# Sums of four key tiles for the softmax denominators, a third score bank, and normalising on GpSimd, in an attention and feed-forward block

## The reference

```
def _tc_rmsnorm(x, t, gw, gb, bw, bb):
    g = (t @ gw.T + gb)[:, None, :]
    b = (t @ bw.T + bb)[:, None, :]
    inv_rms = rsqrt(mean(x * x, axis=-1, keepdims=True) + EPS)
    return g * x * inv_rms + b

def _attention(x, Wq, Wk, Wv, Wo):
    q, k, v = heads of x @ Wq.T, x @ Wk.T, x @ Wv.T
    attn = einsum('blhd,bmhd->bhlm', q, k) / sqrt(dh)
    p = softmax(attn, axis=-1)
    o = einsum('bhlm,bmhd->blhd', p, v).reshape(B, L, D)
    return o @ Wo.T

def _swiglu(x, gate_w, hid_w, out_w):
    return silu(x @ gate_w.T) * (x @ hid_w.T) @ out_w.T

x1 = x + _attention(_tc_rmsnorm(x, t, g1w, g1b, b1w, b1b), Wq, Wk, Wv, Wo)
y  = x + x1 + _swiglu(_tc_rmsnorm(x1, t, g2w, g2b, b2w, b2b), gate_w, hid_w, out_w)
```

## Time and profile before

| | us |
|---|---|
| median of 3 runs | 2556.25 |
| lowest and highest | 2555.16, 2558.97 |
| profiled execution | 2545.35 |
| span of the profiled execution | 2543.2 |

### The profile page before, as it was taken

How to read it: one execution, slowest core, us unless ns; L and a number is a source line. 1 busy time by engine, 2 the same in 40 slices (tenths; PEclk the granted TensorE clock), 3 DMA queues, 4 the chain that set the end, 5 groups by cost and what they waited for, 6 DMA issues and landing times. The chain is left out here.

```text
span 2543.2 us, 39928 instructions
## 1 busy us (share of the span) xinstructions
PE 2382.3 (94%) x11396; PEld 1578.0 (62%) x11396; DVE 1710.1 (67%) x2732; ACT 1310.6 (52%) x2287; POOL 1108.1 (44%) x1063
## 2 busy tenths in 40 slices
PE   5999989999989999989999875999999999999999
PEld 4644436544437444447444344888888888888887
DVE  4766744666735766736667536887787778877877
ACT  3356662556662566653656734436344534453444
POOL 0255551355550555541555534650464147316611
PEclk8999999999999999999999997999999999999999
DMA  6212213212112222132122153115511542154125
GB/s 200 53 40 56 52 30 105 45 43 63 51 31 87 51 52 54 46 92 52 39 53 51 47 166 116 51 33 163 195 57 54 165 166 59 60 173 150 50 75 174
DMA packets 92655, 209.62 MB, mean 82 GB/s; under 512 B 15632, under 2 KB 15632, under 8 KB 90640
## 3 DMA queue, kind: packets, MB, share of 16 engines
q1 hardware_dynamic: 91344, 202.71, 27.2%
q0 software_dynamic: 1088, 4.19, 0.5%
HBM read 134.23 MB, written 19.92 MB: 61 GB/s over the span
## 5 line engine op out<-in xcount | busy, mean ns | idle before, releaser
L410 POOL TENSOR_TENSOR sums<-probs 128x512 f32<-128x512 f32 x512 | 653.3, 1301 | 791.7 <-ACT probs L558 789.2
L632 DVE TENSOR_REDUCE pmax<-bank 128x1 f32<-128x512 f32 x1024 | 654.7, 684 | 282.0 <-PE bank L842 271.0
L558 ACT ACTIVATE probs<-bank 128x512 f32<-128x512 f32 x1024 | 584.5, 597 | 398.7 <-PE bank L926 365.4
L926 PE MATMUL bank<-qs,ks 128*128 128x512 f32 x1024 | 458.0, 452 | 29.2 <-ACT probs L558 28.6
L842 PE MATMUL bank<-ks,qs 96*128 96x512 f32 x1024 | 403.3, 407 | 25.5 <-DVE pmax L632 25.4
L926 PEld LDWEIGHTS bank<-qs,ks 128*128 128x128 f32 x1024 | 191.0, 187 | 369.5 <-ACT probs L558 225.0
L1489 PE MATMUL bank<-H_hi,wt_hi 128*128 128x512 f32 x896 | 350.0, 391 | 14.8 <-DVE H_lo L1344 14.6
L1503 PE MATMUL bank<-ow,aw 128*128 128x512 f32 x1536 | 358.6, 392 | 0.0
L1489 PE MATMUL bank<-H_lo,wt_hi 128*128 128x512 f32 x896 | 349.3, 390 | 0.0
L1489 PE MATMUL bank<-H_hi,wt_lo 128*128 128x512 f32 x896 | 349.3, 390 | 0.0
L1503 PEld LDWEIGHTS bank<-ow,aw 128*128 128x128 f32 x1536 | 285.6, 188 | 59.8 <-issue 1.2
(11 more groups left out here) (135 smaller groups left out, 3138.3 us busy)
## 6 DMA issues: line engine op xcount, KB each, us to landing
raw<-in_gu_w SPq DMA_DIRECT2D x66, 512.0 KB, 3.6
wo_raw<-in_out_w SPq DMA_DIRECT2D x128, 256.0 KB, 2.8
ks<-qk_hi SPq DMA_DIRECT2D x136, 128.0 KB, 2.4
qs<-qk_hi SPq DMA_DIRECT2D x264, 64.0 KB, 2.0
x<-in_x SPq DMA_DIRECT2D x10, 1024.0 KB, 5.7
ks<-qk_lo SPq DMA_DIRECT2D x68, 128.0 KB, 2.4
qs<-qk_lo SPq DMA_DIRECT2D x132, 64.0 KB, 2.0
wv<-wv_parts SPq DMA_DIRECT2D x4, 2048.0 KB, 8.7
```

The lines of the kernel that those rows point to most:

```text
L410: nc.gpsimd.tensor_tensor(sums[:, h, :], probs[:, 0, h, :], probs[:, 1, h, :], ALU.add) \
L558: nc.scalar.activation(probs[:, s % 2, h, :], sbank[i % SB][:], ACT.Exp, scale=SCALE).then_inc(st_done, 1)
L632: nc.vector.reduce_max(pmax[:, t, h, hf:hf + 1], mbank[n % MB][:], AX_X).then_inc(sq_done, 1)
L926: nc.tensor.matmul(sbank[i % SB][:], ks[:, g % 2, h, s * P:(s + 1) * P], qs[:, u % 3, h, :], start=True, stop=True).then_inc(st_ready, 1)
```

## The change

- **Denominators.** GpSimd adds four key tiles before TensorE multiplies with ones: at tiles 1, 2 and 3 of each four (three additions a head, the later ones in place in `sums`), none at the fourth. Two denominator groups a unit take the place of four, without accumulation between them. They are made in the work bank, for the first quad in step 21 (key tile 5, head 1) and for the second in step 5 of the next unit. ScalarE copies the first to `den`; VectorE adds the second from the bank. GpSimd waits with the next sums until TensorE has read the last.
- **Banks.** The bank of the denominators goes, and the scores have three banks.
- **Waits of the exponentials.** An exponential waits for the sum of two tiles before, in three tiles of four.
- **Steps.** Query tiles, key tiles, `hT` tiles and value groups are put at other steps, so that the work bank is free for the denominators.
- **Normalising.** VectorE keeps the two transposes and the reciprocal (tile 3 of the next unit), the multiplication with `o` goes to GpSimd, before the sums of tile 5.
- **VectorE's operands.** ScalarE scales an `hT` tile inside its PSUM bank, and VectorE subtracts from the bank. The rest of the maxima is a reduction with addition over a pair (negated maxima, rounded maxima) where it was a subtraction of two SBUF tiles. The copies of gain and bias are reductions over one element.
- **Output.** The first output tile's copy comes after two splits of `o`, where it came after three and the last normalisation; the last denominators are multiplied after the second output tile, where it was after the first.

The diff, cut to its core:

```diff
-PAIRS = 4
+QUADS = 2
+QT = 4
...
-    PROJECTED.update({("Q", odd + 2): (odd * UNIT, 2), ("K", odd + 3, 0): (odd * UNIT + 18, 2),
+    PROJECTED.update({("Q", odd + 2): (odd * UNIT + 7, 2), ("K", odd + 3, 0): (odd * UNIT + 16, 1),
                       ("K", odd + 3, 1): ((odd + 1) * UNIT, 1), ("Q", odd + 3): ((odd + 1) * UNIT + 9, 2)})
 
-PROJECTED.update({("Q", NU - 1): (5 * UNIT, 2), ("Q", NU): (6 * UNIT, 2), ("K", NU, 0): (7 * UNIT + 16, 2),
+PROJECTED.update({("Q", NU - 1): (5 * UNIT + 7, 1), ("Q", NU): (6 * UNIT + 8, 2), ("K", NU, 0): (7 * UNIT + 15, 1),
                   ("K", NU, 1): (7 * UNIT + 24, 2)})
 
-HT_AT = {5: (10, 14, 18, 22), 7: (0, 4, 8, 12)}
+HT_AT = {5: (12, 15, 18, 24), 7: (0, 2, 8, 11)}
+SUMS_AT = {(5, 1): (0, 0), (1, 1): (1, 1)}
 MAXIMA_AT = (6, 3)
-SB, MB = 2, 3
+VALUES_AT = (3, 1, 3, 2)
+SB, MB = 3, 3
...
+def sums_at(u, s, h):
+    back, quad = SUMS_AT.get((s, h), (NU, 0))
+    return ("D", u - back, quad) if u >= back else None
...
-    obank, dbank, wbank = psum[5], psum[6], psum[7]
+    obank, wbank = psum[6], psum[7]
...
+            def normalise(b, u):
+                pool.wait_ge(od_act, b * NU + (u + 2))
+                pool.wait_ge(den_ready, b * NU + (u + 1))
+                cols = o[:, u // 2, u % 2 * QB:(u % 2 + 1) * QB]
+                nc.gpsimd.tensor_tensor(cols, cols, den[:], ALU.mult).then_inc(on_done, 1)
...
+                        if s == 4 and u:
+                            normalise(b, u - 1)
+                        for h in range(GH if s % QT else 0):
 
                             pool.wait_ge(st_done, SCORES_T(b, NT + n * GH + h + 1) + SB)
-                            if h == 0:
-                                pool.wait_ge(d_ready, products_done(b, u, s // 2))
-                            nc.gpsimd.tensor_tensor(sums[:, h, :], probs[:, 0, h, :], probs[:, 1, h, :], ALU.add) \
+                            if s % QT == 1 and h == 0:
+                                pool.wait_ge(w_ready, MISC(b, sums_before(u, s // QT)))
+                            if s % QT > 1:
+                                pool.wait_ge(sum_done, sums_done(b, u, s - 1, h))
+                            first = probs[:, 0, h, :] if s % QT == 1 else sums[:, h, :]
+                            nc.gpsimd.tensor_tensor(sums[:, h, :], first, probs[:, s % 2, h, :], ALU.add) \
                                 .then_inc(sum_done, 1)
...
-                    nc.scalar.activation(hT_full[:, k, cols], bank[:], ACT.Identity, bias=cur_bias[:, k:k + 1],
+                    nc.scalar.activation(bank[:], bank[:], ACT.Identity, bias=cur_bias[:, k:k + 1],
                                          scale=cur_gain[:, k:k + 1]).then_inc(full, 1)
                     n = hf * KT + k + 1
                     act.wait_ge(full, n if b is None else b * (NHALF * KT) + (NHALF * KT + n))
-                    nc.scalar.activation(hT[0][:, k, cols], hT_full[:, k, cols], ACT.Copy).then_inc(w_act, 1)
+                    nc.scalar.activation(hT[0][:, k, cols], bank[:], ACT.Copy).then_inc(w_act, 1)
                 elif tile[0] == "mT":
                     maxima_rows(tile[1], 0)
+                elif tile[0] == "D":
+                    u = tile[1]
+                    act.wait_ge(on_done, b * NU + (u + 1))
+                    if u == 0:
+                        act.wait_ge(y_stored[1], b * (NT // 2 * 16) + 16)
+                    nc.scalar.activation(den[:], bank[:], ACT.Copy).then_inc(w_act, 1)
...
-                            if s % 2 == 0:
-                                act.wait_ge(sum_done, sums_done(b, u, s // 2 - 1, h) if s
-                                            else sums_done(b, u - 1, PAIRS - 1, h))
+                            if s % QT != QT - 1:
+                                act.wait_ge(sum_done, sums_done(b, u, s - 2, h) if s >= 2
+                                            else sums_done(b, u - 1, NS + s - 2, h))
...
-                    nc.vector.tensor_tensor(hT[1][:, k, cols], hT_full[:, k, cols],
+                    nc.vector.tensor_tensor(hT[1][:, k, cols], bank[:],
                                             hT[0][:, k, cols].bitcast(F32), ALU.subtract).then_inc(w_dve, 1)
+                elif tile[0] == "D":
+                    nc.vector.tensor_tensor(den[:], bank[:], den[:], ALU.add).then_inc(w_dve, 1)
...
-                link(nc.vector.tensor_reduce(mx[:], pmax[:], AX_X, ALU.max, negate=True))
+                dve.wait_ge(mt_ready, b * (2 * NU) + (2 * u + 2))
+                maxima = pmax[:].rearrange("p t h f -> p (t h) f")
+                nc.vector.tensor_reduce(pair[:, 0, :], maxima, AX_X, ALU.max, negate=True).then_inc(dve_step, 1)
+                Link.n += 1
 
                 dve.wait_ge(w_ready, MISC(b, misc_index(True, ("mT", u - 1)) + 1 if u else 0))
                 hi, lo = mt[:, :, 96:96 + 2 * GH:2], mt[:, :, 97:97 + 2 * GH:2]
-                link(nc.vector.tensor_reduce(hi, pmax[:], AX_X, ALU.max, negate=True))
-                nc.vector.tensor_tensor(lo, mx[:], hi.bitcast(F32), ALU.subtract).then_inc(mt_ready, 1)
+                nc.vector.tensor_reduce(hi, pmax[:], AX_X, ALU.max, negate=True).then_inc(mt_ready, 1)
+                link(nc.vector.tensor_reduce(pair[:, 1, :].bitcast(F32R), maxima, AX_X, ALU.max))
+                with nc.allow_low_precision(reason="the rest of the maxima is rounded as its matmul operand"):
+                    nc.vector.tensor_reduce(lo, pair[:].rearrange("p a (t h) -> p t h a", h=GH), AX_X,
+                                            ALU.add).then_inc(mt_ready, 1)
...
-                g, hf = u // 2, u % 2
                 if part == 0:
-                    dve.wait_ge(od_act, b * (2 * NU) + (2 * (u + 1) + 2))
+                    dve.wait_ge(w_dve, MISC_DVE(b, dve_before(True, ("D", u, 1)) + 1))
 
                     link(nc.vector.transpose(den[:], den[:]))
                 elif part == 1:
                     cols = den[:].rearrange("p (c i) -> p c i", i=32)
-                    link(nc.vector.reciprocal(dsmall[:], cols[:, :, 0]))
-                elif part == 2:
-                    link(nc.vector.transpose(den[:], dsmall[:].unsqueeze(2).to_broadcast([P, QB // 32, 32])))
+                    link(nc.vector.reciprocal(pair[:, 1, :], cols[:, :, 0]))
                 else:
-                    cols = o[:, g, hf * QB:(hf + 1) * QB]
-                    nc.vector.tensor_tensor(cols, cols, den[:], ALU.mult).then_inc(on_done, 1)
+                    nc.vector.transpose(den[:], pair[:, 1, :].unsqueeze(2).to_broadcast([P, QB // 32, 32])).then_inc(den_ready, 1)
...
-                            nc.vector.tensor_copy(cur_gain[:], gain[:, bass.ds(nb, 1), :].squeeze(1)).then_inc(const_dve, 1)
-                            nc.vector.tensor_copy(cur_bias[:], bias[:, bass.ds(nb, 1), :].squeeze(1)).then_inc(const_dve, 1)
+                            nc.vector.tensor_reduce(cur_gain[:], gain[:, bass.ds(nb, 1), :].rearrange("p b k -> p k b"), AX_X,
+                                                    ALU.max).then_inc(const_dve, 1)
...
-                for t in range(3):
+                for t in range(2):
                     lo_part(t)
-                for part in range(4):
+                out_tile(0)
+                for t in range(2, 4):
+                    lo_part(t)
+                work_tile(b, ("D", NU - 1, 1))
+                for part in range(3):
                     normalise(b, NU - 1, part)
-                for t in range(NT):
+                for t in range(1, NT):
                     out_tile(t)
...
-            def denominators(b, u, pair):
-                pe.wait_ge(sum_done, sums_done(b, u, pair, GH - 1))
-                if pair == 0:
-                    pe.wait_ge(od_act, b * (2 * NU) + (2 * u + 2))
+            def denominators(b, u, quad):
+                work_bank_empty(b, ("D", u, quad))
+                pe.wait_ge(sum_done, sums_done(b, u, QT * quad + QT - 1, GH - 1))
                 for h in range(GH):
-                    last = nc.tensor.matmul(dbank[DH * h:DH * h + DH, :], ones[:], sums[:, h, :], start=(pair == 0),
-                                            stop=(pair == PAIRS - 1))
-                last.then_inc(d_ready, 1)
+                    last = nc.tensor.matmul(wbank[DH * h:DH * h + DH, :], ones[:], sums[:, h, :], start=True, stop=True)
+                last.then_inc(w_ready, 1)
...
-                            if h == 2 + (s + 1) % 2 and (u or s):
+                            if h == VALUES_AT[s % QT] and (u or s):
                                 values(b, u if s else u - 1, (s - 1) % NS)
-                                if s % 2 == 0:
-                                    denominators(b, u if s else u - 1, (s // 2 - 1) % PAIRS)
+                            if sums_at(u, s, h):
+                                denominators(b, *sums_at(u, s, h)[1:])
...
-                    if t == 0:
-                        denominators(b, NU - 1, PAIRS - 1)
+                    if t == 1:
```

(22 more changed lines are left out.)

60 lines of the change are left out of this document (29 added, 31 removed).

## The result

| | before | after |
|---|---|---|
| median of 4 runs, us | 2557.61 (2555.16 to 2559.71) | 2518.95 (2513.37 to 2527.12) |
| profiled execution, us (span) | 2545.35 (2543.2) | 2516.71 (2514.9) |
| granted clock, mean | 0.984 | 0.971 |

The ratio is 0.9857 [0.9832, 0.9881]: the change gains 39 us, where the forecast of 2460 meant 98. Of the 39, the two profiled executions show 29; the other 10 are that the profiled execution of before lay 12 us under its median and that of after 2 under its own.

A forecast was written before the change was run, and what follows sets the result against it. Bound: TensorE's content plus its handover with ScalarE through two score banks. Half units summed to 114 us saved over four batches, minus 28 for imperfect overlap, plus 5 for output: net 91, 2454 profiled; predicted 2460, range 2420 to 2525.

The forecast's parts named there:

- Denominators: TensorE's denominator groups go from 128 to 64, each one removed saving 0.86 us: 55 us, all on the path.
- Third bank: Three score banks loosen the TensorE-ScalarE handover; waits fall from 4.4 us a unit to nearly nothing.
- GpSimd's cycle of 16.1: Twelve sums (14.9 us), denominator matmuls and restart form a closed cycle of 16.1 us a half unit, 32.2 a unit.
- First half of a batch, 21.8: First score to first denominator group's end: 5.8 us to tile 1's first exponential, then 14.9 + 1.1.
- DMA wait of the keys: In units 1 and 3 ScalarE's key copy waits some 3.7 us for query DMAs, making that half unit 20.0 us.
- Rival C: The DMA wait does not bite and half units are as tight as the cycle: 2420 us; chance 14%.
- The halves behind, 16.6: The two half units after those with the DMA wait: TensorE 16.1 us and a wait for the maxima.
- From unit 6 to 7, 17.1: Second half unit of unit 6: 17.1 us, with an inverse root of 1.02 us on GpSimd.
- VectorE without two SBUF operands: Fewer VectorE instructions and GpSimd sums hold each other up: 0 to 10 us by itself; sums stay at 1.24.
- normalising, free: GpSimd's one multiplication a unit (1.28 us) hides under the denominator group: nothing to +0.1 us.
- Rival B: Only the removed matmuls count: 55 us gives 2500, down to half of that, 2530; chance 16%.
- Rival D: GpSimd is a brake: sums at 1.55 us would make units 39.6 us and the kernel 2617; chance 4%.

The follow-up runs named there:

- two_banks: The changed kernel with two score banks instead of three, nothing else: 2538.86 us, ratio 0.9949.
- half_sums: The changed kernel with GpSimd's sums over 256 of each tile's 512 columns, half the denominators' additions left out; one execution: 2465.47 us.
- fewer_query_dmas: The changed kernel with 8 of the 12 DMAs issued for query tiles made in units 1 and 3; one execution: 2490.68 us.
- port_free: The changed kernel with the scaling and variances of the next batch's tokens moved from VectorE to ScalarE: 2507.84 us, ratio 0.982.
- all_edits: The changed kernel with units 1 and 3's first key half at step 22, scaling and variance on ScalarE, unit 7's transposes later: 2480.29 us, ratio 0.971.
- scale_on_act: The changed kernel with next-batch token scaling moved from VectorE to ScalarE, unit 6's mean square and inverse root one tile earlier: 2529.86 us, ratio 0.9899.

## Why the prediction was wrong

Its sign and its range held. Its size did not: by the profiled executions 2454 was forecast and 2516.7 measured, 63 us more. **The step that failed is the sum of the half units**: it gave each the GpSimd cycle of 16.1 us or a count that left out terms on TensorE and ScalarE. Where the 63 us are, over four batches: the first half 4 x 3.7 = 15; the halves with the DMA wait 18; the ones behind them 18; the second group of unit 4, 6; unit 5, 4; from unit 6 to 7, 23; the rest -2. That is 83 (with rounding), of which 28 had been put in as slop. The remaining 8 are the lead (1.6), the output stages, which gained 1.2 and not 5, 2 behind the batches, and rounding.

*Denominators*: right. 512 records fewer and 64 groups, the gain on TensorE's queue as counted.

*Third bank*: right in kind, mis-sized. "The waits of a unit would fall from 4.4 to nearly nothing": it is worth 20 us (two_banks), since GpSimd's cycle then bounds half of the halves and projections the rest.

*GpSimd's cycle of 16.1*: right in size, and half_sums shows that it bounds. Two steps in it failed. "The wait of an exponential for a sum two tiles back is met with over 1 us to spare": it occurs 159 times, 89.9 us, as exponentials take 0.60 us each and can come four at a time, and sums 1.24. The bound therefore acts through this wait, and the denominator group itself waits only 24 times. And the halves with projections (16.1 by the sum) are 16.8, which half_sums leaves as they are. The slop of 0.5 us a half was not needed in regular ones.

*First half of a batch, 21.8*: wrong, it was counted by ScalarE and GpSimd alone. half_sums left it at 25.5, so it is not GpSimd's. Adding TensorE's work again, with 32 maxima in 25 steps and 1.1 for each value group, as the prediction priced it elsewhere, gives 23.6; 1.9 stay open.

*DMA wait of the keys*: the mechanism was forecast and found, 4.9 instead of 3.7 us. From the end of the query tile's projection (499.5) to the keys' copy (511.0) it is 11.5 instead of 10.4 us: SyncE's row of twelve issues took 7.7 us instead of 6.9, as one took 1.40, and the query tile's copy began 0.2 us late. TensorE took 6.8 us between the two projections, as forecast (6.7); ScalarE was idle from 0.2 us before the second ended. The end of the query tile came 8.0 us into the half instead of 7.2. Where the clock fell already before the denominator group (unit 3 of batch 1, 2.7 us at half clock) the half is 23.0 and not 21.9. Rival C, that the wait would not bite, is out.

*The halves behind, 16.6*: mis-sized, and not by the clock (fewer_query_dmas has 18.8 with none at half clock). TensorE's content was to be 16.1; the order in time has beside it 0.65 us for the copy of `o` at the unit's start, 0.4 at the transpose of the maxima, about 0.1 more on each first step behind a long block, and 1.1 for exponentials in the last step. None of the four had been added. half_sums takes the last away and leaves 18.1 to 18.6 us. There the shorter halves are those with less half clock (1.1 to 1.4 us in 18.1 and 18.2, 2.7 to 3.4 in 18.6): where the exponentials do not hold the half, the clock seems to cost; that was not tested by itself.

*From unit 6 to 7, 17.1*: GpSimd's cycle and an inverse root were counted, and not TensorE's path through the work bank. It took 22.2 to 24.2. There two tiles of hT are transposed into the one bank two steps apart, and the denominator group needs it next. In the trace after, the first tile waits 2.29 us for the scaling and the second 1.34 for the first one's rest, and the value products and the group then run at half clock (1.94 + 1.82 instead of 1.06 + 1.07 us). port_free, where nothing waits for VectorE's scaling, still has 20.9 to 22.6: its trace shows 4 of the 23 us gone. With shorter sums (half_sums) it is 18.0 to 18.4, and with the transposes further apart (all_edits) 17.2 to 17.9, of which 2 us come back in the next half. How the rest splits between the bank, GpSimd and the clock was not separated.

*VectorE without two SBUF operands, "0 to 10 us"*, and *normalising, free*: here the mechanism was wrong. The prediction counted as disturbed only instructions with two SBUF inputs. Rows 7 and 8 could not show more, as GpSimd paused after every four sums then. Under rows of 8 to 12 sums, instructions from SBUF to SBUF with one fp32 input wait too: scaling (0.88 to 1.50 us each instead of 0.48), the variance (0.92 to 4.65 instead of 0.15 to 0.17). The Trainium skill ("VectorE: DVE Perf Modes", section "Mode 2×_2P — use both read ports for one tensor") gives fp32 tensor_scalar and tensor_copy, from SBUF to SBUF, a mode that takes both of VectorE's read ports. The trace agrees for tensor_scalar, the form of both instructions, while transposes (0.70) and reductions (0.68) kept their time. port_free takes both away and gives 11 us in all.

*The same part in the other direction*: "VectorE loses a multiplication of 1.11 us, which is on no path". In its old place it is worth 89 us beside the longer sums; four reductions later between 1 and 7. The loss of 19 us that the prediction worked out for the move from GpSimd's longer instruction did not come. So the part was not a cost or a gain of its own, but necessary beside the longer sums unless the instruction moves.

*Rival B* (2500 to 2530) gave the right time by luck: the halves that it said would not shrink did (16.2, 16.8), and others grew. *Rival D* is out: sums stayed at 1.29 to 1.31.

## What to carry to other kernels

When an engine's short bursts become one long row, list what the other engines do from the same memory during it, instructions of 4 elements too. Here VectorE's instructions from SBUF to SBUF paid between the rest of one GpSimd sum and the rest of the whole row, and not a factor on their own time; so put them where the row ends. A lower clock behind a wait is not yet a cost: compare the stretch up to the next common wait with a run at full clock. And a content sum must be made for each kind of half unit, the first included, by the engine with the most work in it.

## What the runs showed of the hardware

While GpSimd adds, VectorE's instructions from SBUF to SBUF end at a fixed distance behind the end of one of GpSimd's: a multiplication of 128x512 0.55 us behind it (0.69 us alone), a scaling of 128x512 0.28 (0.48 alone), a variance of 128x4 0.03 (0.15 alone). Which end it is differs. The four scalings of unit 6 of the changed kernel ended behind the first four sums of a row of eight, one behind each, and the sum after each took 1.44 or 1.45 us instead of 1.27. Long multiplications went past the ends of two sums (up to 4.04 us). The variance of scale_on_act went past three and ended behind the fourth instruction, a multiplication that ended at 697.95 and after which GpSimd paused (4.64 us). Reductions from a bank (0.68 us) and the 32x32 transposes from SBUF to SBUF (0.70) kept their time. A sum over 256 columns takes 0.74 us and one over 512 takes 1.31, so by an estimate from these two some 0.17 of each is not the columns'. SyncE needs 0.51 to 1.40 us for each DMA that it issues here; twelve in a row take 7.7 us, the longest step of the keys' way.
